# Post-norm transformer layer with a top-2 mixture of experts on one core: two more pieces of a small per-batch chain moved from VectorE to GpSimd

## The chip, the cores and the metric

One Trainium2 chip, one of its cores. The time is the kernel's device time in microseconds. The engines are named as in the profile: PE (TensorE matrix products), PEld (its weight loads), DVE (VectorE), ACT (ScalarE), POOL (GpSimd) and SP (SyncE, which issues most DMAs).

## The reference

```python
x = layernorm(x + attn(x))      # x: (4, 1024, 128), 16 heads of 8, rotary Q and K, causal softmax, W_O
p = softmax(x @ Wg + bg)        # 8 experts; the two largest are kept and divided by their sum
h = gelu(x @ W1[e] + b1[e]);  y = h @ W2[e] + b2[e]
x = layernorm(x + sum over the two experts of gate * y)
```
`layernorm(x) = (x - mean) / sqrt(var + 1e-5)`, without scale or shift. Everything is float32.

## The kernel before, in words

Tokens are handled in four batches of 1024 (`B = 4`), each as `BT = 8` tiles of 128 tokens, one token to a partition. Attention runs over 16 units: four batches, and in each four groups of four heads (`NG = 4`). A unit has 12 steps (`NB = 12`, `B_STEPS`): a step is one block of keys by up to 512 queries.

One list of events, `EVENTS` from `schedule()`, sets the order of the work on every engine: each engine walks the same list and issues its own part of each event. Behind step k of unit u stand two `QK` events (scores of the next step; PE, then ACT's exponential at L894, then on the diagonal steps 0 to 3 and 8 to 11 POOL's mask, L1499), `A` events of the next unit (a first pass over the scores: PE writes one of three PSUM banks of a ring, L723 to L728, and DVE reduces it to row maxima, L1203), and `PV` of the step before (probabilities by values, PE L778), which needs the masks of its own step. `SPLIT` cuts the row maxima into three bf16 parts on POOL (L1431 to L1437); `MT` transposes them on PE (L738). The ring has three banks, so PE can be at most three items ahead of DVE.

While the units of batch bt + 1 run, the small work that follows attention of batch bt is placed behind its steps by `after(bt)`, one event to a step. What matters here, with bt from 0 to 2 on POOL and DVE:

- `LNM`: DVE takes mean and variance pieces (`bn_stats`, L1288). `LNV`: POOL turns them into `mean` and `dev` (`moments`, L951 to L960 and L1461), behind step 9.
- `LNR` 0 and 1, behind steps 10 and 11: DVE finds `rstd = 1/sqrt(var)` with a first guess from the bits (`root_start`, L1043 and L1045) and three rounds of Newton's rule (`root_step`, L1050, L1052, L1054); one round in `LNR` 0, two in `LNR` 1. `LNR` 1 lies behind the unit's last `A` items and its `SPLIT`.
- `LNA` 0 and 1, behind steps 0 and 1 of the next unit: POOL normalises four tiles each (L998). `T2` 0 and 1, behind steps 2 and 3: PE transposes the normalised tiles (L819); `T2` c waits for `LNA` c (`x1_done`). `LG` is the gate's product (L794).
- `RD`, `RE`: POOL writes token names (L992) and running sums of the ranks (L966 to L971). `RF` 0 and 1, behind steps 4 and 5 two units on, is `place`: `RF` 0 on POOL makes each token's row for each expert (L978 to L982), `RF` 1 on DVE picks the two chosen experts' rows, with a product and a sum over eight experts each (L985, L986), and casts them (L987). `VX` copies values (L1414).
- `SC`: POOL sends the tokens to their rows in DRAM with 16 indirect DMAs (L1485), one behind each following step; the first waits for `slots_ready`.

The last batch's chain runs later, under the experts' tiles, and stays on DVE. All engines issue in order; a wait of one instruction holds all that is queued behind it on its engine. Batches 0 and 1 run in a hardware loop, batch 2 behind it.

## Time and profile before

| | us |
|---|---|
| median of 3 runs (800.60 to 803.19) | 802.84 |
| the profiled execution | 794.03 |
| its span | 792.2 |
| PE busy in the span | 661.1 (83%) |
| DVE busy | 567.6 (72%) |
| ACT busy | 442.5 (56%) |
| POOL busy | 352.9 (45%) |

The rows are from the profiled execution. The span is the stretch that the trace covers; 1.8 us of that execution's time lie outside it. Times in a row are from the span's start.

### The profile page before, as it was taken

The numbers are of one execution on the slowest core, as the hardware profiler recorded it, in microseconds if no ns is written. First come the engines' busy times: TensorE is split into PE (matmuls) and PEld (weight loads), VectorE is DVE, ScalarE is ACT, GpSimd is POOL, SyncE is SP. The second block draws the span as 40 slices with busy tenths as digits, with TensorE's granted clock in tenths as the row PEclk, the third lists the DMA queues.
The fourth block names the chain that finished last, engine by engine and source line by source line (L and its number), as shares of the span: only waits on it lengthen the run. The fifth ranks groups of instructions, "written<-read, shape, count | busy, mean of one in ns | idle before, by whom it ended". The sixth has DMA issues, their size and how long they took to land.

```text
span 792.2 us, 19057 instructions
## 1 busy us (share of the span) xinstructions
PE 661.1 (83%) x5560; PEld 355.8 (45%) x5561; DVE 567.6 (72%) x1386; ACT 442.5 (56%) x840; POOL 352.9 (45%) x664
## 2 busy tenths in 40 slices
PE   7879999999798997989999998898699666999830
PEld 3344333334343333434333334332298666889720
DVE  8977888888879886787988897986256622222266
ACT  2343667666565675456567656567467333566514
POOL 5862223323344484152447526248423654434551
PEclk9986999999999998898999999999799887999985
DMA  8883455011010120101012101000277645787923
GB/s 288 278 279 132 145 152 156 5 48 49 2 50 3 58 82 17 49 3 48 14 50 80 40 21 48 2 7 32 79 218 198 199 128 149 196 223 204 322 68 106
DMA packets 67358, 83.75 MB, mean 106 GB/s; under 512 B 9266, under 2 KB 46776, under 8 KB 67264
## 3 DMA queue, kind: packets, MB, share of 16 engines
q1 hardware_dynamic: 62912, 74.04, 31.6%
q0 software_dynamic: 4352, 8.53, 3.1%
q8 instruction: 49, 0.80, 0.4%
q14 instruction: 45, 0.37, 0.2%
HBM read 55.77 MB, written 26.90 MB: 104 GB/s over the span
## 4 chain that ended last, share of the span: by engine, by line
PE 50%; DVE 21%; issue 11%; SPq 7%; ACT 5%; POOL 2%; DMA 2%; another core or an unknown queue 1%; DVEq 0%; ACTq 0%; POOLq 0%
PE banks L778 15%; DVE mx L1203 12%; PE banks L728 9%; PE banks L758 6%; PE banks L847 4%; PE banks L836 4%; PE banks L723 3%; ACT region L894 2%; PE banks L670 2%; PE banks L787 2%; SPq L611 2%; SPq L612 2%; SPq L605 1%; DMA region<-pairs 1%
## 5 line engine op out<-in xcount | busy, mean ns | idle before, releaser
L1203 DVE TENSOR_REDUCE mx<-banks 128x1 f32<-128x512 f32 (+3 forms) x640 | 364.9, 630 | 49.9 <-PE banks L728 44.8
L894 ACT ACTIVATE region<-banks 128x1024 f32<-128x1024 f32 (+3 forms) x256 | 201.4, 841 | 134.6 <-PE banks L758 130.0
L728 PE MATMUL banks<-region 64*128 64x512 bf16 (+3 forms) x768 | 186.4, 337 | 13.6 <-DVE mx L1203 10.6
L758 PE MATMUL banks<-region 64*128 64x512 bf16 (+3 forms) x768 | 138.3, 338 | 12.4 <-ACT region L894 5.7
L778 PE MATMUL banks<-region 128*32 128x512 f32 (+3 forms) x1024 | 117.7, 533 | 0.9 <-POOL region L1499 0.8
L1509 POOL DMA_INDIRECT results<-region,dest x72 | 71.7, 995 | 102.4 <-DVE region L1335 74.7
L894 ACT ACTIVATE cs_sb<-banks 128x1024 f32<-128x1024 f32 (+2 forms) x128 | 91.0, 759 | 42.9 <-PE banks L758 42.5
L723 PE MATMUL banks<-mask_sb,half_sb 64*128 64x128 bf16 (+1 forms) x384 | 82.2, 247 | 25.2 <-DVE mx L1203 19.8
L1499 POOL TENSOR_SCALAR_AFFINE_SELECT region<-region 128x256 f32<-128x256 f32 x160 | 64.1, 409 | 82.5 <-ACT region L894 79.2
L847 PE MATMUL banks<-region,w1e 128*128 128x128 f32 x576 | 81.7, 287 | 21.0 <-ACT region L922 17.3
L1329 DVE TENSOR_TENSOR region<-banks,w1e 128x128 f32<-128x128 f32 x72 | 20.9, 291 | 108.6 <-PE banks L836 58.3
L1499 POOL TENSOR_SCALAR_AFFINE_SELECT cs_sb<-cs_sb 128x256 f32<-128x256 f32 x96 | 38.3, 410 | 127.6 <-ACT cs_sb L894 126.8
L758 PEld LDWEIGHTS banks<-region 64*128 64x128 bf16 x768 | 42.1, 94 | 111.9 <-issue 39.9
L836 PE MATMUL banks<-w_sb,region 128*128 x576 | 81.0, 285 | 4.5 <-issue 2.4
L728 PEld LDWEIGHTS banks<-region 64*128 64x128 bf16 x768 | 62.7, 97 | 49.1 <-DVE mx L1203 35.1
L847 PEld LDWEIGHTS banks<-region,w1e 128*128 128x128 f32 x576 | 74.1, 201 | 23.3 <-ACT region L922 18.9
L930 ACT ACTIVATE region<-banks,w1e 128x128 f32<-128x128 f32 x288 | 82.8, 378 | 0.5 <-PE banks L847 0.5
L836 PEld LDWEIGHTS banks<-w_sb,region 128*128 128x128 f32 x576 | 71.9, 195 | 9.1 <-issue 7.6
L1485 POOL DMA_INDIRECT pairs<-xT_sb,slot x64 | 63.2, 987 | 24.3 <-issue 14.6
L922 ACT COPY region<-banks 128x128 f32<-128x128 f32 x72 | 19.2, 267 | 90.5 <-PE banks L856 60.7
L725 PE MATMUL banks<-mask_sb,half_sb 64*128 64x64 bf16 (+1 forms) x384 | 69.2, 205 | 0.0
L723 PEld LDWEIGHTS banks<-mask_sb,half_sb 64*128 64x128 bf16 x384 | 34.6, 96 | 62.7 <-DVE mx L1203 45.5
(201 smaller groups left out, 700.8 us busy)
## 6 DMA issues: line engine op xcount, KB each, us to landing
w1e<-in_w SPq DMA_DIRECT2D x72, 322.0 KB
region<-stack_q SPq DMA_DIRECT2D x64, 112.0 KB
region<-stack_k SPq DMA_DIRECT2D x32, 224.0 KB
region<-pairs SPq DMA_DIRECT2D x72, 66.0 KB
region<-results SPq DMA_DIRECT2D x8, 512.0 KB, 4.7
stack_q<-x_sb SPq DMA_DIRECT2D x8, 384.0 KB, 3.5
stack_k<-x_sb SPq DMA_DIRECT2D x8, 384.0 KB, 4.6
stack_q<-x_sb SPq DMA_DIRECT2D x8, 256.0 KB, 3.6
```

Of the source, the lines that this page charges most:

```text
L723: mm(view[:, :, n - P:n], half_sb[rows, 0, :], mask_sb[rows, 0, 0:k, :], start=True, stop=False, skip_group_check=True)
L725: mm(view[:, :, n - P // 2:n], half_sb[rows, 1, :], mask_sb[rows, 1, 0:k, P // 2:P], start=False, stop=False, skip_group_check=True)
L728: last = mm(ring[:, bank, m * n:(m + 1) * n], qst[rows, v % NG, sb_ // 4, slot_, sb_ % 4 * P:(sb_ % 4 + 1) * P], kst[rows, v % NG, slot_, ...
L758: last = mm(score[:, slot_, par, 0:n], kst[rows, u % NG, slot_, j * P:(j + 1) * P], qst[rows, u % NG, c, slot_, s0 - c * CH:s0 - c * CH + ...
L778: last = mm(pv[32 * h:32 * h + 32, s0 - c * CH:s0 - c * CH + n], vx[:, u % NG, j, h, :], probs[(2 * e[1] + slot_) % 6][:, par, 0:n], start ...
L836: last = mm(down[k % 2], hg[:, k % 2, hc * P:(hc + 1) * P], w2_sb[:, bass.ds(e, 1), hc, :].rearrange("p a n -> p (a n)"), start=(hc == 0), ...
L847: last = mm(hidden[k % 2][:, hc * P:(hc + 1) * P], w1e[:, k, hc * P:(hc + 1) * P], xgT[:, k % 2, :], start=(hc == 0), stop=(hc == HC - 1), ...
L894: nc.scalar.activation(probs[i % 6][:, :, 0:n], score[:, i % 2, :, 0:n], ACT.Exp, scale=SCALE).then_inc(exp_done, 1)
L930: nc.scalar.activation(hg[:, k % 2, cols], hidden[k % 2][:, cols], ACT.Gelu_apprx_tanh, bias=w1e[:, k, HID + hc:HID + hc + 1]).then_inc(ge ...
L1203: read(v.tensor_reduce(dst, src, AX.X, ALU.max, negate=True))
L1499: pp.affine_select(out=block_, in_=block_, compare_op=ALU.is_ge, fill=0.0, base=0, pattern=[[0, 2], [1, P]], channel_multiplier=-1).then_i ...
L1509: pp.indirect_dma_start(out=results, out_offset=bass.IndirectOffsetOnAxis(ap=dest[:, k, :], axis=0), in_=ys[:, k, :], in_offset=None, boun ...
```

## The change

For batches 0 to 2 the Newton rounds of `LNR` 0 and 1 and the whole of `RF` 1 are issued by POOL. `root_start` stays on DVE. POOL has no fused form of the rounds here, so a round is four instructions where DVE had three; and the sum over eight experts is three additions of halves where DVE had one reduction. The counts of the semaphores `ln`, `route`, `pool_ln` and `pool_route` follow; `LNA` 0 now waits for `pool_ln`, and `TA` (tables of the experts' tiles) also for `pool_route`. The order of events is unchanged.

```diff
@@ place
                 for w in range(2):
-                    chain(v.tensor_tensor(rt[:, 8, :, :], rt[:, 6 + w, :, :], row, ALU.mult))
-                    chain(v.tensor_reduce(slot_f[:, w, :], rt[:, 8, :, :], AX.X, ALU.add))
+                    mine = rt[:, 8, :, :]
+                    chain(v.tensor_tensor(mine, rt[:, 6 + w, :, :], row, ALU.mult))
+                    if v is nc.vector:
+                        chain(v.tensor_reduce(slot_f[:, w, :], mine, AX.X, ALU.add))
+                    else:
+
+                        chain(v.tensor_tensor(mine[:, :, 0:4], mine[:, :, 0:4], mine[:, :, 4:8], ALU.add))
+                        chain(v.tensor_tensor(mine[:, :, 0:2], mine[:, :, 0:2], mine[:, :, 2:4], ALU.add))
+                        chain(v.tensor_tensor(slot_f[:, w, :], mine[:, :, 0], mine[:, :, 1], ALU.add))
                 v.tensor_copy(slot[:, :, :], slot_f[:, :, :]).then_inc(slots_ready, 1)
@@ DVE, LNR
+                    elif half == 1 and bt < B - 1:
+                        return
                     else:
                         sync()
                         if half == 0:
                             if bt < B - 1:
-                                ve.wait_ge(pool_ln, at((bt + 1) * 8, 8))
+                                ve.wait_ge(pool_ln, at(bt * POOL_LN + 8, POOL_LN))
                             root_start(rstd[:, :], dev[:, 1, :], step, sync)
-                        for _ in range(1 + half):
-                            root_step(rstd[:, :], dev[:, 1, :], nwt[:, :], step, sync)
...
@@ DVE, ROUTE_STEPS: "RF": (0, 4) becomes "RF": (0, 0)
@@ POOL
+                    elif kind == "LNR":
+                        if half == 0:
+
+                            pool.wait_ge(ln, at((bt + 1) * (BT + 2), BT + 2))
+                            pool.sem_inc(mask_turns, 1)
+                        for _ in range(1 + half):
+                            link(pp.tensor_tensor(nwt[:, :], rstd[:, :], rstd[:, :], ALU.mult))
+                            link(pp.tensor_tensor(nwt[:, :], nwt[:, :], dev[:, 1, :], ALU.mult))
+                            link(pp.tensor_scalar(nwt[:, :], nwt[:, :], -0.5, 1.5, ALU.mult, ALU.add))
+                            link(pp.tensor_tensor(rstd[:, :], rstd[:, :], nwt[:, :], ALU.mult))
...
                     if c == 0:
                         pool.wait_ge(xr_free, at(bt + 1, 1))
-                        pool.wait_ge(ln, at((bt + 1) * (BT + 11), BT + 11))
+                        pool.wait_ge(pool_ln, at((bt + 1) * POOL_LN, POOL_LN))
```

POOL's instructions at the norm of batch 2, before (`affine_select` is the mask; `L998` rows are `LNA`):

```order
L1461 TENSOR_SCALAR dev<-dev 128x8 [waits pool_ln]
L1499 AFFINE_SELECT cs_sb<-cs_sb 128x2x128 [waits exp_done] x2
L1499 AFFINE_SELECT region<-region 128x2x128 [waits exp_done] x2
L1431 TENSOR_TENSOR msp<-mx,zero 128x2x8 [waits mx_ready]
L1433 TENSOR_TENSOR mrem<-mx,msp 128x2x2x4 [waits msplit]
L1435 TENSOR_TENSOR msp<-mrem,zero 128x2x8 [waits msplit]
L1437 TENSOR_TENSOR msp<-mrem,msp 128x2x8 [waits msplit]
L1499 AFFINE_SELECT region<-region 128x2x128 [waits exp_done] x2
L998 TENSOR_SCALAR xT_sb<-y,mean,rstd 128x128 [waits xr_free,ln]
L998 TENSOR_SCALAR xT_sb<-y,mean,rstd 128x128 x3
L1499 AFFINE_SELECT cs_sb<-cs_sb 128x2x128 [waits exp_done] x2
L998 TENSOR_SCALAR xT_sb<-y,mean,rstd 128x128 x4
```

and of the change, the same place (here L1519 is the mask, L1441 to L1447 the split, L1008 the normalisation):

```order
L1519 AFFINE_SELECT cs_sb<-cs_sb 128x2x128 [waits exp_done] x2
L1478 TENSOR_TENSOR nwt<-rstd 128x8 [waits ln]
...
L1481 TENSOR_TENSOR rstd<-rstd,nwt 128x8 [waits pool_ln]
L1519 AFFINE_SELECT region<-region 128x2x128 [waits pool_ln,exp_done]
...
L1478 TENSOR_TENSOR nwt<-rstd 128x8
L1479 TENSOR_TENSOR nwt<-nwt,dev 128x8 [waits pool_ln]
...
L1481 TENSOR_TENSOR rstd<-rstd,nwt 128x8 [waits pool_ln]
L1519 AFFINE_SELECT region<-region 128x2x128 [waits pool_ln,exp_done]
...
L1008 TENSOR_SCALAR xT_sb<-y,mean,rstd 128x128 [waits xr_free,pool_ln]
```

Four instructions now stand between POOL's masks of step 11 and those of the next unit's step 0, and eight between the split and the masks of step 1, with both `LNA` behind them.

DVE's instructions at the same place before:

```order
L1045 TENSOR_SCALAR rstd<-rstd 128x8 [waits ln]
L1050 TENSOR_TENSOR nwt<-rstd 128x8 [waits ln]
L1052 SCALAR_TENSOR_TENSOR nwt<-nwt,dev 128x8 [waits ln]
L1054 SCALAR_TENSOR_TENSOR rstd<-nwt,rstd 128x8 [waits ln]
L1203 TENSOR_REDUCE mx<-banks 128x1 [waits ring_full,ln]
L1203 TENSOR_REDUCE mx<-banks 128x1 [waits ring_full]
L1207 TENSOR_TENSOR mx<-mx 128x4x4 [waits ring_read]
L1050 TENSOR_TENSOR nwt<-rstd 128x8 [waits ln]
...
L1054 SCALAR_TENSOR_TENSOR rstd<-nwt,rstd 128x8 [waits ln]
L1203 TENSOR_REDUCE mx<-banks 128x2 [waits ring_full,ln]
```

and of the change:

```order
L1053 TENSOR_SCALAR rstd<-dev 128x8 [waits pool_ln,ln]
L1055 TENSOR_SCALAR rstd<-rstd 128x8 [waits ln]
L1214 TENSOR_REDUCE mx<-banks 128x1 [waits ring_full,ln]
L1214 TENSOR_REDUCE mx<-banks 128x1 [waits ring_full]
L1218 TENSOR_TENSOR mx<-mx 128x4x4 [waits ring_read]
L1214 TENSOR_REDUCE mx<-banks 128x2 [waits ring_full] x4
L1221 COPY mparts<-banks 48x128 [waits ring_full]
```

The nine instructions of the rounds are gone; the reductions close up.

POOL's instructions at the places of batch 2 in the change (before, the first indirect DMA followed the copy directly, and the product, reduction and cast were DVE's):

```order
L985 TENSOR_TENSOR next_row<-next_row,cnt 128x8 [waits pool_route]
L1424 COPY region<-v_sb 128x32x8 [waits pool_route,vx_set,pv_done]
L989 TENSOR_TENSOR xT_sb<-xT_sb 128x64
L994 TENSOR_TENSOR xT_sb<-xT_sb 128x8x4 [waits pool_route]
L995 TENSOR_TENSOR xT_sb<-xT_sb 128x8x2 [waits pool_route]
L996 TENSOR_TENSOR slot_f<-xT_sb 128x8 [waits pool_route]
L989 TENSOR_TENSOR xT_sb<-xT_sb 128x64 [waits pool_route]
...
L996 TENSOR_TENSOR slot_f<-xT_sb 128x8 [waits pool_route]
L997 CAST slot<-slot_f 128x16 [waits pool_route]
L1505 DMA pairs<-xT_sb,slot 34816x132 [waits x1_copied,slots_ready]
```

Nine instructions stand ahead of the first indirect DMA.

## Rows read from the trace of the kernel before

**Rows 1.** Page, part 4: the chain that ended last, shares by engine.
```profile
PE 50%; DVE 21%; issue 11%; SPq 7%; ACT 5%; POOL 2%; DMA 2%; another core or an unknown queue 1%; DVEq 0%; ACTq 0%; POOLq 0%
```
**Rows 2.** Windows: PE, PEld, DVE, ACT, POOL busy us (instructions), clock, DMA share, GB/s.
```profile
228.00:338.00 110.00, 97.71 (x862) 39.41 (x862) 90.63 (x193) 66.31 (x90) 46.30 (x110) 0.95 0.13 41
...
218.20:226.10 7.90, 7.90 (x75) 3.41 (x74) 5.94 (x13) 3.23 (x6) 7.44 (x12) 0.78 0.17 48
```
**Rows 3.** Timeline, POOL, norm of batch 0: start, us, line, operation, [idle before].
```profile
212.25 0.20 POOL L960 TENSOR_TENSOR dev<-dev 128x8 f32<-128x8 f32 x1 [0.18 <-POOL dev L958]
212.64 0.20 POOL L1461 TENSOR_SCALAR dev<-dev 128x8 f32<-128x8 f32 x1 [0.20 <-POOL dev L960]
...
213.54 0.41 POOL L1499 TENSOR_SCALAR_AFFINE_SELECT region<-region 128x256 f32<-128x256 f32 x1
...
216.07 0.22 POOL L1431 TENSOR_TENSOR msp<-mx,zero 128x16 bf16<-128x16 f32 x1 [1.28 <-DVE mx L1207]
...
217.16 0.76 POOL L1499 TENSOR_SCALAR_AFFINE_SELECT region<-region 128x256 f32<-128x256 f32 x2
217.92 3.15 POOL L998 TENSOR_SCALAR xT_sb<-y,mean,rstd 128x128 f32<-128x128 f32 x4
...
221.79 3.12 POOL L998 TENSOR_SCALAR xT_sb<-y,mean,rstd 128x128 f32<-128x128 f32 x4
```
**Rows 4.** Timeline, DVE, the same stretch.
```profile
213.29 0.33 DVE L1045 TENSOR_SCALAR rstd<-rstd 128x8 int32<-128x8 int32 x1
213.65 0.32 DVE L1050 TENSOR_TENSOR nwt<-rstd 128x8 f32<-128x8 f32 x1
...
214.49 1.29 DVE L1203 TENSOR_REDUCE mx<-banks 128x1 f32<-128x512 f32 x2
...
215.91 0.16 DVE L1050 TENSOR_TENSOR nwt<-rstd 128x8 f32<-128x8 f32 x1
...
217.24 1.95 DVE L1203 TENSOR_REDUCE mx<-banks 128x2 f32<-128x256 f32 x4
```
**Rows 5.** Timeline, PE: transposes of the row maxima, and of `LNA` 0 and 1.
```profile
218.56 0.26 PE L738 MATMUL banks<-idb_sb,msp 128*96 128x128 bf16 x1
...
224.17 0.60 PE L819 MATMUL banks<-id_sb,xT_sb 128*128 128x128 f32 x4
...
226.10 0.66 PE L819 MATMUL banks<-id_sb,xT_sb 128*128 128x128 f32 x4
```
**Rows 6.** Chain in order of time, behind the second transpose.
```profile
226.17 0.59 PE banks L819 x4
...
228.22 0.69 DVE mx L1203
```
**Rows 7.** Timeline, POOL and PE, the norm of batch 2.
```profile
484.89 3.13 POOL L998 TENSOR_SCALAR xT_sb<-y,mean,rstd 128x128 f32<-128x128 f32 x4
...
489.12 0.66 PE L819 MATMUL banks<-id_sb,xT_sb 128*128 128x128 f32 x4
```
**Rows 8.** Timeline, all engines, the places of batch 0.
```profile
263.62 0.32 POOL L981 TENSOR_TENSOR xT_sb<-xT_sb,next_row 128x64 f32<-128x64 f32 x1 [0.18 <-POOL xT_sb L980]
...
264.11 0.21 POOL L982 TENSOR_TENSOR next_row<-next_row,cnt 128x8 f32<-128x8 f32 x1 [0.18 <-POOL xT_sb L981]
...
264.72 0.40 POOL L1414 COPY region<-v_sb 128x256 f32 x1 [0.40 <-POOL next_row L982]
...
265.97 0.21 DVE L985 TENSOR_TENSOR xT_sb<-xT_sb 128x64 f32<-128x64 f32 x1
...
267.07 2.49 DVE L1203 TENSOR_REDUCE mx<-banks 128x1 f32<-128x512 f32 x4
...
267.82 0.28 PE L723 MATMUL banks<-mask_sb,half_sb 64*128 64x256 bf16 x1 [0.90 <-DVE mx L1203]
...
268.12 1.21 POOL L1485 DMA_INDIRECT pairs<-xT_sb,slot  x1 [3.00 <-DVE slot L987]
...
271.60 0.40 POOL L1499 TENSOR_SCALAR_AFFINE_SELECT cs_sb<-cs_sb 128x256 f32<-128x256 f32 x1 [2.27 <-ACT cs_sb L894]
```

More of the change, by code:

```diff
@@ L454, in build @@
         pool_ln = sem("pool_ln")
-        POOL_ROUTE = 13
+        POOL_STEPS = {("LNV", 0): 0, ("LNR", 0): 8, ("LNR", 1): 12,
+                      ("RD", 1): 0, ("RE", 0): 2, ("RE", 1): 5, ("RF", 0): 9, ("RF", 1): 13}
+        POOL_LN, POOL_ROUTE = 20, 21
         spare_in = sem("spare_in")
@@ L1110, in early_tiles @@
                 ve.wait_ge(route, 2 + (B - 1) * PER_ROUTE)
+                ve.wait_ge(pool_route, (B - 1) * POOL_ROUTE)
                 chain(v.tensor_tensor(n_e, next_row[:, :], first_row_sb[:, :], ALU.subtract))
@@ L1175, in late_tiles @@
                                            tile_at[:, EARLY:NTILE], ALU.mult, ALU.add).then_inc(tiles_ready, 1)
-            ROUTE_STEPS = {"RA": (1,), "RS": (3,), "RB": (3, 3), "RC": (3, 2), "RD": (5, 0), "RE": (0, 0), "RF": (0, 4)}
+            ROUTE_STEPS = {"RA": (1,), "RS": (3,), "RB": (3, 3), "RC": (3, 2), "RD": (5, 0), "RE": (0, 0), "RF": (0, 0)}
             LAST_STEPS = {**ROUTE_STEPS, "RD": (5, 2), "RE": (3, 4), "RF": (4, 4)}
             PER_ROUTE = sum(sum(n) for n in ROUTE_STEPS.values())
-            PER_LN = BT + 5 + 6
+            PER_LN = BT + 2
             def visit(e, r, at):
@@ L1265, in visit @@
                     else:
-                        if bt < B - 1:
-                            ve.wait_ge(pool_route, at((bt + 1) * POOL_ROUTE, POOL_ROUTE))
                         place(v, half, link_route)
@@ L1276, in visit @@
                     bt, half = e[1:]
-                    done = [bt * PER_LN + {"LNM": half * BT // 2, "LNV": BT, "LNR": BT + (bt == B - 1) * 8 + half * 5}[kind]]
+                    done = [bt * PER_LN + {"LNM": half * BT // 2, "LNV": BT, "LNR": BT + (bt == B - 1) * (8 + half * 5)}[kind]]
                     def step(ins):
@@ L1298, in visit @@
                             if bt < B - 1:
-                                ve.wait_ge(pool_ln, at((bt + 1) * 8, 8))
+                                ve.wait_ge(pool_ln, at(bt * POOL_LN + 8, POOL_LN))
                             root_start(rstd[:, :], dev[:, 1, :], step, sync)
-                        for _ in range(1 + half):
-                            root_step(rstd[:, :], dev[:, 1, :], nwt[:, :], step, sync)
-                    if kind == "LNR" and half == 1:
-                        assert done[0] == (bt + 1) * PER_LN + (bt == B - 1) * 8
+                        if bt == B - 1:
+                            for _ in range(1 + half):
+                                root_step(rstd[:, :], dev[:, 1, :], nwt[:, :], step, sync)
                 elif kind == "TA":
@@ L1437, in visit @@
                     pp.tensor_tensor(part[2], rest, part[1], ALU.subtract).then_inc(msplit, 1)
-                elif e[0] in ("LNV", "RD", "RE", "RF") and e[1] < B - 1 and (e[0] in ("LNV", "RE") or e[2] == (e[0] == "RD")):
+                elif e[0] in ("LNV", "LNR", "RD", "RE", "RF") and e[1] < B - 1 and (e[0], *e[2:]) != ("RD", 0):
                     kind, bt, half = e
-                    turn, per, first = (pool_ln, 8, 0) if kind == "LNV" else (
-                        pool_route, POOL_ROUTE, {("RD", 1): 0, ("RE", 0): 2, ("RE", 1): 5, ("RF", 0): 9}[kind, half])
+                    turn, per = (pool_ln, POOL_LN) if kind in ("LNV", "LNR") else (pool_route, POOL_ROUTE)
+                    first = POOL_STEPS[kind, half]
                     done = [bt * per + first]
@@ L1456, in visit @@
                     if kind == "LNV":
-                        pool.wait_ge(ln, at(bt * (BT + 11) + BT, BT + 11))
+                        pool.wait_ge(ln, at(bt * (BT + 2) + BT, BT + 2))
                         pool.sem_inc(mask_turns, 1)
@@ L1461, in visit @@
                         step(pp.tensor_scalar(dev[:, 1, :], dev[:, 0, :], 1.0 / D, EPS, ALU.mult, ALU.add))
+                    elif kind == "LNR":
+                        if half == 0:
+                            pool.wait_ge(ln, at((bt + 1) * (BT + 2), BT + 2))
+                            pool.sem_inc(mask_turns, 1)
+                        for _ in range(1 + half):
+                            link(pp.tensor_tensor(nwt[:, :], rstd[:, :], rstd[:, :], ALU.mult))
+                            link(pp.tensor_tensor(nwt[:, :], nwt[:, :], dev[:, 1, :], ALU.mult))
+                            link(pp.tensor_scalar(nwt[:, :], nwt[:, :], -0.5, 1.5, ALU.mult, ALU.add))
+                            link(pp.tensor_tensor(rstd[:, :], rstd[:, :], nwt[:, :], ALU.mult))
                     elif kind == "RD":
```

## The prediction

> **What bounds the kernel now.** I read the page's chain of work first. PE holds half of it and DVE a fifth, POOL 2% [rows 1]: through attention PE and DVE take turns, tied by the ring of three banks, and between two norms PE is busy 97.71 and DVE 90.63 of 110 us [rows 2]. Neither has much idle time in which a delay could be made up. So I read the two places of the change in order of time on POOL, DVE and PE, and ask at each which engine is waited for.
>
> At the norm of batch 0 DVE's rounds lie in front of reductions that PE waits for. One round runs from 213.65 to the next reduction at 214.49, two from 215.91 to 217.24 [rows 4]: 0.84 and 1.33 us, 2.17 in all. POOL meanwhile waits 1.28 us before its split at 216.07, and from there it is without a gap: split, masks, four normalisations from 217.92 to 221.07, masks, four more from 221.79 to 224.91 [rows 3]. PE transposes the second four at 226.10 [rows 5], 1.19 us after POOL is done with them. That 1.19 us is all the cover that POOL's queue has there. In the chain in order of time that transpose is PE's own, and behind it come PE's gate product, scores and first pass, and then DVE's reduction at 228.22 [rows 6]. A delay of the transpose is a delay of what follows.
>
> At the places of batch 0 DVE's five instructions run from 265.97 to 267.07, and PE has waited 0.90 us for the reduction behind them when it goes on at 267.82 [rows 8]. POOL has been done with its copy since 265.12 and waits for the cast; its first indirect DMA starts at 268.12, its next mask at 271.60 [rows 8].
>
> **The change part by part. 1. DVE loses nine instructions at each norm.** They are on the path: PE could go on up to 2.17 us sooner, so taken alone this is worth up to 6.5 us in three batches. The price of DVE's dropped register and wait work is in those gaps already.
>
> **2. POOL gains four instructions behind the masks of step 11.** POOL has no Newton round in this trace. The nearest rows are the last steps of the variance, same size (128x8), same engine, same kind of wait behind each: 0.20 us long, but 212.25 to 212.64 from start to start [rows 3], 0.39 us. I price a step at 0.40. The multiply-add and the last step are of the same kind. `root_start` ends at 213.62 [rows 4]; four steps from 213.7 end, wait included, at 215.3. The pair of masks that stood at 213.54 and behind then takes 0.75 us, to 216.05. The split stood at 216.07 and had waited 1.28 us for DVE. DVE is now earlier, POOL is not: the split stays where it was. So these four steps cost nothing, covered by that 1.28 us and by the gap between the two masks; they also use up all of it, so DVE's earlier maxima bring POOL nothing. What the masks hold up, PE's products of the next unit's step 0, comes behind 218.56 [rows 5].
>
> **3. POOL gains eight instructions behind the split.** They depend on each other: 8 x 0.40 = 3.2 us. Queued behind them are the masks of step 1, `LNA` 0, the masks of step 2, `LNA` 1, the masks of step 3. No idle time stands between these before [rows 3], so all shift by 3.2: `LNA` 0 ends at 224.25 instead of 221.07, `LNA` 1 at 228.1 instead of 224.91. PE came to the first transpose at 224.17 and to the second at 226.10 [rows 5]. The first is hardly later than before, though PE comes sooner and waits. The second goes from 226.10 to 228.2, 2.1 us later than before. In batch 2 the same sum gives 484.89 + 3.13 + 3.2 = 491.2 against 489.12 [rows 7], again 2.1; batch 1 lies like batch 0. Hence the gain of part 1 is gone, eaten by waits of PE between 217 and 228, and 3 x 2.1 = 6.3 us are lost on top. Bounds: if POOL's steps followed each other at their length alone (0.20), the eight would take 1.6 and the transpose be 0.4 late, 1.2 us in all; if each took 0.5, as POOL's 128x64 step does from start to start (263.62 to 264.11) [rows 8], 4.0 us, a lateness of 2.9, 8.7 in all. I take 0.40, whose rows have the size and the waits of the new steps.
>
> The Trainium skill bears on this choice: Perfetto Trace Analysis, section GPSIMD Engine Instruction, says that a GpSimd span in a profile is unreliable and that such instructions should be timed from start to start. By spans the three batches would lose 1.2 us, by starts 6.3; the trace agrees with the page in so far as its start-to-start time is twice the span [rows 3].
>
> **4. The places.** DVE loses 1.10 us (265.97 to 267.07). PE's own work ends at about 266.9, 0.90 us before it goes on [rows 8], so 0.9 of it is a gain, 2.7 us in three batches (bounds 0, if another wait takes its place, and 3.3). POOL gains nine instructions. Two products of 128x64 at 0.49 from start to start, two sums of 32 at about 0.45 (between the rows for 64 and for 8 elements, as an estimate), four more at 0.40, a cast of 0.2: 3.7 us [rows 3, 8]. From 265.12 they end near 268.8, 1.7 us later than DVE's cast. The indirect DMA follows by 0.97 us as before and takes 1.21 [rows 8]: it ends near 271.0, ahead of the mask that stood at 271.60 and comes at 270.7 now. The mask is some 0.3 us late; its product on PE is some steps away. So it costs nothing; without that cover it would be 0.3 a batch.
>
> **5. Semaphores.** `TA` waits for `pool_route` too, which was met long before. Nothing.
>
> **The sum.** +6.3 - 2.7 = +3.6 us on the profiled execution's 794.03, so 797.6. The median of the runs shown, 802.84, is 8.8 above that execution; the change is the same number of microseconds on it: 806.4. A measurement here can tell about 0.3%, 2.4 us, from no change.
>
> **The rivals.**
> **A. The forecast**: PE's second transpose waits for `LNA` 1, the places gain. +2.4 to +6.5 us, 805.2 to 809.3. Chance 0.50.
> **B. The clock makes it worse.** In the 7.9 us up to the second transpose PE's granted clock was 0.78 [rows 2]: a mix of 2.4 and 1.2 GHz, about 3.5 us at the lower level (0.22 x 2 x 7.9), behind DVE's rounds and PE's waits for them. Those 3.5 us now lie in time that PE waits anyway. But PE's new waits come later, up to 228.2, and if the lower level moves behind the transpose it costs up to half of 3.5, 1.7 us a batch. For it: from 216.2 to 228.2 PE has about 6.2 us of work at full clock (0.78 x 7.9), so it idles half of the time. Against: from 228 to 338, with 12 us of PE's waits in it, the clock is 0.95 on the mean [rows 2]. +3.6 + 5.2 = +8.8, 811.6. Chance 0.17.
> **C. POOL's steps are as short as their spans**, or the chain is otherwise short: +1.2 - 2.7 = -1.5, 801.3. Also here, with the same time, that PE's part behind the transpose has slack of its own. Chance 0.15.
> **D. Faster: the lateness is recovered.** The 2.1 us arise at one place; the next place where this chain matters is 40 us later. If DVE, not PE, sets the pace in between, the ring fills while PE waits, and PE's lateness is absorbed by the 12 us that PE is idle in 110 [rows 2]. Then only the places count: -2.7, 800.1. It decides for "faster" if fewer than 0.1 us of each 2.1 are left. Against it: during the wait DVE has nothing to reduce either, since PE issues the first pass behind the transpose, and the chain there is all PE. Chance 0.11.
> **E. The work moved, but the path doesn't notice**: PE waits elsewhere for the same things. Within 2.4 us of 802.8. Chance 0.07.
>
> **How the numbers follow.** Slower holds A and B, 0.67, and a little of C and E's tails, 0.69. Within 0.3% are most of C and E and the edge of A: 0.18. Faster is D and the tail of C, 0.13. The range leaves out the far end of B and of D: 800.6 to 811.5. A's own range is 805.2 to 809.3.
>
> **What the changed profile would show.** POOL: four L1478 to L1481 steps near 213.7, 0.4 apart; the split still near 216.1; eight steps to 220.4; `LNA` 1 ending near 228.1. PE: waits at the masks of step 1 and at both transposes, the second released by POOL's L1008, near 228.2 in the time of before. DVE: reductions without a gap from 213.65, then idle between 221 and 228. At the places: PE's 0.90 us wait gone, the first indirect DMA near 269.8. Right size: the start of the same step of batch 1 later by 1.2 us than before. The prediction is wrong if PE's second transpose is not released by POOL, if the steps' spacing is not 0.4, or if the distance from that transpose to the places shrinks.

## The result and the profile after

The changed kernel takes 810.85 us (median of 4 runs, 810.06 to 814.17) against 801.78 us (4 runs, 800.60 to 803.19) for the kernel before in the same comparison. The ratio is 1.0127, 95% interval [1.0087, 1.0166]: slower by 7 to 13 us, where +3.6 us was forecast. The profiled execution took 810.95 us, with a span of 809.1.

The page of the changed kernel, busy time and chain of work (the lines that answer to [rows 1] and the small table):
```profile
PE 680.4 (84%) x5560; PEld 368.1 (45%) x5561; DVE 562.6 (70%) x1344; ACT 443.7 (55%) x840; POOL 366.4 (45%) x727
...
PE 51%; DVE 17%; issue 9%; SPq 5%; ACT 5%; POOL 5%; another core or an unknown queue 3%; DMA 2%; POOLq 0%; DVEq 0%; ACTq 0%
```
DVE's share of the chain fell from 21 to 17%, as its instructions left. POOL's rose from 2 to 5%. PE is busy 19 us longer with the same number of matmuls, and its mean granted clock is 0.913 instead of 0.933; the windows below show where it was lower.

POOL of the changed kernel in order of time, norm of batch 0 (start, us, line, [idle before]). All that stands here is 3.96 us late already when the norm begins (DVE's L1055 starts at 217.24, its counterpart of before at 213.29 [rows 4]); those 3.96 us arose between 45 and 75 us, ahead of every edit of the change, where the changed kernel's clock was at its lower level for 34 us in all and that of the kernel before for 17. Other kernels below show between -0.2 and +4.4 there whatever was edited. The 3.96 us are taken off in what follows.
```profile
217.75 0.20 POOL L1478 TENSOR_TENSOR nwt<-rstd 128x8 f32<-128x8 f32 x1 [0.21 <-DVE rstd L1055]
218.13 0.20 POOL L1479 TENSOR_TENSOR nwt<-nwt,dev 128x8 f32<-128x8 f32 x1 [0.18 <-POOL nwt L1478]
...
219.58 0.76 POOL L1519 TENSOR_SCALAR_AFFINE_SELECT region<-region 128x256 f32<-128x256 f32 x2 [0.33 <-POOL rstd L1481]
220.31 0.22 POOL L1441 TENSOR_TENSOR msp<-mx,zero 128x16 bf16<-128x16 f32 x1
...
221.37 0.20 POOL L1478 TENSOR_TENSOR nwt<-rstd 128x8 f32<-128x8 f32 x1
...
224.06 0.20 POOL L1481 TENSOR_TENSOR rstd<-rstd,nwt 128x8 f32<-128x8 f32 x1 [0.18 <-POOL nwt L1480]
224.58 0.76 POOL L1519 TENSOR_SCALAR_AFFINE_SELECT region<-region 128x256 f32<-128x256 f32 x2 [0.33 <-POOL rstd L1481]
225.34 3.15 POOL L1008 TENSOR_SCALAR xT_sb<-y,mean,rstd 128x128 f32<-128x128 f32 x4
...
229.21 3.11 POOL L1008 TENSOR_SCALAR xT_sb<-y,mean,rstd 128x128 f32<-128x128 f32 x4
```
The split starts at 220.31, less 3.96 that is 216.35, against 216.07 [rows 3]: where it stood. The steps are 0.38 us apart, from 221.37 to 224.06 in seven of them. The second normalisation ends at 232.32 - 3.96 = 228.36.

PE of the changed kernel, its waits in the same stretch:
```profile
221.47 0.33 PE L741 MATMUL banks<-idb_sb,msp 128*96 128x128 bf16 x1 [0.96 <-POOL msp L1447]
...
228.55 0.66 PE L822 MATMUL banks<-id_sb,xT_sb 128*128 128x128 f32 x4 [1.30 <-POOL xT_sb L1008]
...
232.38 0.66 PE L822 MATMUL banks<-id_sb,xT_sb 128*128 128x128 f32 x4 [1.77 <-POOL xT_sb L1008]
```
Both transposes are released by POOL, and the second starts at 228.42 in the time of before, 2.32 us later than at 226.10 [rows 5].

And the chain of the changed kernel in order of time, through the second transpose:
```profile
226.93 1.56 POOL xT_sb L1008 x2
228.49 0.73 POOL cs_sb L1519 x2
229.22 3.12 POOL xT_sb L1008 x4
232.33 0.04 issue
232.38 0.66 PE banks L822 x4
233.03 0.79 PE banks L797 x8
```
POOL's queue carries the chain where it was PE's own before [rows 6].

What the forecast left out lies behind that transpose. Windows of the changed kernel (columns as in [rows 2]): the stretch with the two waits, then one behind the second transpose of each of the three batches:
```profile
226.00:232.40 6.40, 3.32 (x32) 1.38 (x24) 3.21 (x7) 2.03 (x4) 6.40 (x11) 1.00 0.40 129
235.20:242.00 6.80, 6.76 (x40) 3.54 (x40) 4.64 (x9) 3.57 (x5) 1.27 (x5) 0.50 0.01 1
368.30:378.50 10.20, 10.20 (x58) 5.83 (x57) 6.05 (x12) 6.04 (x7) 1.49 (x6) 0.50 0.00 0
501.40:511.60 10.20, 10.20 (x56) 4.47 (x53) 5.95 (x14) 5.07 (x7) 1.22 (x5) 0.50 0.01 2
```
and of the kernel before: its stretches at the lower level ahead of the norm's transposes in batches 0 and 1, and what it does where the changed kernel is slow:
```profile
219.00:222.40 3.40, 3.40 (x30) 1.16 (x26) 1.80 (x5) 1.42 (x4) 3.40 (x6) 0.50 0.04 8
229.00:235.80 6.80, 6.32 (x59) 3.28 (x63) 6.25 (x15) 5.62 (x8) 1.27 (x5) 1.00 0.08 28
352.10:355.50 3.40, 3.40 (x32) 1.55 (x30) 2.76 (x6) 1.70 (x3) 3.40 (x6) 0.50 0.01 2
365.80:372.60 6.80, 6.72 (x33) 1.97 (x33) 5.03 (x12) 3.33 (x5) 0.00 (x0) 0.50 0.02 4
489.50:499.70 10.20, 9.37 (x83) 4.80 (x81) 8.81 (x19) 8.70 (x11) 1.22 (x5) 1.00 0.14 45
```
PE is busy 3.32 of 6.40 us up to the second transpose, at a granted clock of 1.00; then, with PE full of work again, the clock is 0.50, that is 1.2 GHz, for 6.8, 10.2 and 10.2 us. In 10.2 us PE gets through 56 matmuls where it did 83.

To see where each microsecond arose I matched the matmuls of L778 (L781 in the changed kernel), probabilities by values, one by one in the order in which they run: 1536 in either trace. The shift is the start in one trace minus the start in the trace of before. Times on the left are those of before.

| changed kernel, shift in us | norm 0 | norm 1 | norm 2 |
|---|---|---|---|
| ahead of the norm (212.6, 346.6, 475.9) | 3.96 | 5.44 | 8.32 |
| at the second transpose | 6.27 | 7.87 | 10.66 |
| 14 to 25 us behind it (240.2, 385.5, 511.9) | 8.73 | 9.06 | 14.37 |
| ahead of and behind the places | 8.58, 7.88 | 8.92, 8.21 | 14.37, 13.67 |

So in these two traces a norm costs 2.31, 2.43 and 2.34 us up to the transpose, 7.1 in all, and 2.46, 1.19 and 3.71 behind it, 7.4 in all. In batch 1 the kernel before has a stretch at the lower level of its own there (365.80, above), worth 2.45 us (by so much run 3's shift falls there, and nothing else of it changes). The places give back 0.70 each, 2.1 us. Sum: +12.3 us, inside the measured 7 to 13. Not in this sum is a stretch between the norms: from 300 to 334 the shift of the changed kernel falls by 2.5 us, and that of run 2 below, whose norm is DVE's, by 3.0. There the kernel before was at the lower level for 10.2 us (from 311.1), the changed one for 6.8 (from 317.1). Over the whole stretch from 212.6 to 540 the shift grows by 9.7 us. How much of the 7.4 us belongs to this pair of executions alone is taken up behind the last experiment.

### The profile page after: what moved, and what is told of

Read it like the earlier page. It is cut to its first block, busy times and chain, and to the rows that moved or that the text cites. A ratio compares the mean times of both kernels' runs of the same rounds, so it can differ in the third digit from the quotient of the medians.

```text
span 809.1 us, 19151 instructions
## 1 busy us (share of the span) xinstructions
PE 680.4 (84%) x5560; PEld 368.1 (45%) x5561; DVE 562.6 (70%) x1344; ACT 443.7 (55%) x840; POOL 366.4 (45%) x727
## 4 chain that ended last, share of the span: by engine, by line
PE 51%; DVE 17%; issue 9%; SPq 5%; ACT 5%; POOL 5%; another core or an unknown queue 3%; DMA 2%; POOLq 0%; DVEq 0%; ACTq 0%
PE banks L781 14%; DVE mx L1214 11%; PE banks L731 9%; PE banks L761 6%; PE banks L850 4%; PE banks L839 4%; PE banks L673 3%; ACT region L897 3%; PE banks L726 3%; POOL xT_sb L1008 2%; PE banks L790 2%; PE banks L688 2%; SPq L614 2%; SPq L608 1%
## 5 line engine op out<-in xcount | busy, mean ns | idle before, releaser
L731 PE MATMUL banks<-region 64*128 64x512 bf16 (+3 forms) x768 | 191.2, 347 | 11.6 <-DVE mx L1214 8.9
L761 PE MATMUL banks<-region 64*128 64x512 bf16 (+3 forms) x768 | 140.1, 341 | 11.3 <-ACT region L897 5.5
L781 PE MATMUL banks<-region 128*32 128x512 f32 (+3 forms) x1024 | 118.7, 537 | 1.9 <-POOL region L1519 1.8
L1519 POOL TENSOR_SCALAR_AFFINE_SELECT region<-region 128x256 f32<-128x256 f32 x160 | 63.6, 408 | 86.0 <-ACT region L897 81.8
L850 PE MATMUL banks<-region,w1e 128*128 128x128 f32 x576 | 84.2, 293 | 19.8 <-ACT region L925 11.9
L1519 POOL TENSOR_SCALAR_AFFINE_SELECT cs_sb<-cs_sb 128x256 f32<-128x256 f32 x96 | 38.0, 408 | 127.6 <-ACT cs_sb L897 126.6
L839 PE MATMUL banks<-w_sb,region 128*128 x576 | 83.8, 291 | 4.2 <-issue 2.1
L850 PEld LDWEIGHTS banks<-region,w1e 128*128 128x128 f32 x576 | 76.8, 207 | 22.1 <-ACT region L925 13.5
L839 PEld LDWEIGHTS banks<-w_sb,region 128*128 128x128 f32 x576 | 74.6, 201 | 8.8 <-issue 7.7
```

The source lines that it names most:

```text
L731: last = mm(ring[:, bank, m * n:(m + 1) * n], qst[rows, v % NG, sb_ // 4, slot_, sb_ % 4 * P:(sb_ % 4 + 1) * P], kst[rows, v % NG, slot_, ...
L761: last = mm(score[:, slot_, par, 0:n], kst[rows, u % NG, slot_, j * P:(j + 1) * P], qst[rows, u % NG, c, slot_, s0 - c * CH:s0 - c * CH + ...
L781: last = mm(pv[32 * h:32 * h + 32, s0 - c * CH:s0 - c * CH + n], vx[:, u % NG, j, h, :], probs[(2 * e[1] + slot_) % 6][:, par, 0:n], start ...
L839: last = mm(down[k % 2], hg[:, k % 2, hc * P:(hc + 1) * P], w2_sb[:, bass.ds(e, 1), hc, :].rearrange("p a n -> p (a n)"), start=(hc == 0), ...
L850: last = mm(hidden[k % 2][:, hc * P:(hc + 1) * P], w1e[:, k, hc * P:(hc + 1) * P], xgT[:, k % 2, :], start=(hc == 0), stop=(hc == HC - 1), ...
L1519: pp.affine_select(out=block_, in_=block_, compare_op=ALU.is_ge, fill=0.0, base=0, pattern=[[0, 2], [1, P]], channel_multiplier=-1).then_i ...
```

## The experiments

Theories on record with them: **C** (clock), the second transpose is late by POOL's eight steps, and PE's waits for it bring a stretch at 1.2 GHz behind it that costs as much again; **W**, the extra is another wait that POOL's queue brings. All ratios are to the kernel before on the same chip, with 95% intervals. "Shift" is that of the table above. The diffs are excerpts: the semaphore counts that follow an edit are left out.

**1. The rounds on POOL alone.** `RF` 1 goes back to DVE:
```diff
-            ROUTE_STEPS = {"RA": (1,), "RS": (3,), "RB": (3, 3), "RC": (3, 2), "RD": (5, 0), "RE": (0, 0), "RF": (0, 0)}
+            ROUTE_STEPS = {"RA": (1,), "RS": (3,), "RB": (3, 3), "RC": (3, 2), "RD": (5, 0), "RE": (0, 0), "RF": (0, 4)}
```


> Only the Newton rounds are POOL's; the places' second half is DVE's again. Theory C (the clock): the second transpose of each norm comes 2.3 us late, and the lower PE clock that follows PE's waits costs a further 1.3 to 3.7 us behind it. So all of the loss and 2.1 us more: 809 + 2 = about +11 us against the kernel before (1.012 to 1.016). Theory W (a further wait, not the clock, and partly from the places on POOL): the norm alone costs the 6.3 us of the recorded sum, +6 us (1.008), with the lower clock no longer than before.

Measured: 814.95 us, ratio 1.0188 [1.0148, 1.0229], 12 to 18 us slower. Shifts: -0.19, 2.11 and 6.17 at norm 0; 5.03, 7.44, 8.59; 8.65, 11.25, 14.63; nothing at the places. The loss is the norm's. The ratio lies above what theory C expected (1.012 to 1.016), and its interval reaches into it; lateness and extra behind the transposes add up to 7.3 + 8.6 us in the trace.

**2. The places on POOL alone.** The rounds go back to DVE.

> Only the places' second half is POOL's; the Newton rounds are DVE's again. Both theories: DVE drops 1.1 us a batch, of which PE gets 0.7, so -2.1 us (0.997), the norms as in the kernel before. If the places add a hidden cost (the rival that blames them), the ratio is 1.00 or above.

Measured: 798.27 us, ratio 0.9934 [0.9900, 0.9969]. The shift falls by 0.71, 0.71 and 0.70 at the three places, 2.1 us; the ratio says 2.5 to 8. The two parts add up: 1.0188 and 0.9934 make 1.0122, the whole is 1.0127. The ratio gives more than the 2.1 us that can be seen; by the medians, 798.27 against 800.54, it is 2.3. The norms, though, are not as in the kernel before, as was expected: at norm 0 this kernel's shift grows by 4.0 us (3.98 to 7.95), with DVE's rounds and no wait of PE at either transpose. Windows of this kernel, ahead of the second transpose of norm 0 (231.54) and through it, then behind it:
```profile
228.70:235.50 6.80, 6.44 (x65) 3.84 (x57) 5.09 (x11) 4.85 (x6) 1.73 (x7) 1.00 0.35 118
235.50:242.30 6.80, 6.80 (x36) 3.00 (x36) 4.07 (x11) 3.47 (x5) 0.44 (x2) 0.50 0.01 2
```
So a stretch at the lower level behind the transpose, worth 2.5 us (5.44 to 7.95), comes without POOL's steps too, in one of three norms here as in the kernel before. A stretch there is by itself no proof of theory C; how often it comes, and what filling PE's waits does to it, has to decide.

**3. One round on POOL, two on DVE**, where POOL's four steps lie under cover and none stands behind the split:
```diff
-                elif e[0] in ("LNV", "LNR", "RD", "RE", "RF") and e[1] < B - 1 and (e[0], *e[2:]) != ("RD", 0):
+                elif e[0] in ("LNV", "LNR", "RD", "RE", "RF") and e[1] < B - 1 and (e[0], *e[2:]) not in (("RD", 0), ("LNR", 1)):
```


> First Newton round on POOL (the four steps that POOL's idle time covered), rounds two and three on DVE, places on POOL. If part 2 of the prediction is right that four steps are covered: the second transpose is not late, DVE gains 0.84 us at each norm and PE 0.7 at each of the places: -3 to -4.5 us (0.994 to 0.996). If four steps already cost, it is slower than e2.

Measured: 794.72 us, ratio 0.9921 [0.9890, 0.9953], a little faster than the expected 0.994 to 0.996. The second transposes are not late (shifts 2.58 to 2.30, -1.63 to -1.81, -4.92 to -4.97), and behind them there is no stretch at the lower level. DVE in that trace:
```profile
217.65 0.17 DVE L1218 TENSOR_TENSOR mx<-mx 128x16 f32<-128x16 f32 x1
217.93 0.17 DVE L1060 TENSOR_TENSOR nwt<-rstd 128x8 f32<-128x8 f32 x1
218.13 0.17 DVE L1062 SCALAR_TENSOR_TENSOR nwt<-nwt,dev 128x8 f32<-128x8 f32 x1
218.33 0.32 DVE L1064 SCALAR_TENSOR_TENSOR rstd<-nwt,rstd 128x8 f32<-128x8 f32 x1
218.68 0.33 DVE L1060 TENSOR_TENSOR nwt<-rstd 128x8 f32<-128x8 f32 x1
```
DVE now waits for POOL's round until 217.93 and two of its steps take twice as long, so of the 0.84 us that the first round had cost [rows 4] at most 0.3 are won (0.28, 0.18 and 0.05 at the three norms). This is the fastest kernel here, but not measurably faster than the one with the places alone.

**4. PE kept at work while it waits.** The changed kernel, with matmuls whose result nobody reads ahead of the transposes, into the bank that the transposes then fill:
```diff
                     else:
+                        if bt < B - 1:
+                            for _ in range((5, 7)[c]):
+                                mm(ring[:, bank, :], idb_sb[:, :], mask_sb[:, :, :, :].rearrange("p a b n -> p (a b n)"),
+                                   start=True, stop=True, skip_group_check=True)
                         pe.wait_ge(x1_done, at(2 * bt + c + 1, 2))
```


> The changed kernel with 5 and 7 products without use (bf16, 512 columns, into the bank that the transpose then overwrites) ahead of the two transposes that wait for the norm, in batches 0 to 2. They fill PE's waits of 1.3 and 1.8 us and take no time from other work. Theory C: the clock stays at 2.4 GHz behind the transpose, and each norm loses 2.3 us instead of 3.6 to 6.1: +5 us against the kernel before (1.005 to 1.007), 4 to 7 us below the changed kernel. Theory W: as the changed kernel, or slower by the filling.

Measured: 805.29 us, ratio 1.0040 [1.0011, 1.0070]. More work for PE and 0.87% faster than the changed kernel. The second transpose is as late as before (2.32, 2.43, 2.25 us), as it must be, since POOL does the same. Behind it:
```profile
233.20:240.00 6.80, 6.80 (x35) 2.65 (x36) 4.37 (x12) 3.04 (x4) 0.06 (x1) 0.50 0.02 4
366.90:377.10 10.20, 9.32 (x84) 5.19 (x84) 8.38 (x18) 8.19 (x10) 1.98 (x7) 1.00 0.02 6
499.50:506.30 6.80, 6.80 (x36) 2.66 (x36) 4.29 (x12) 3.02 (x4) 0.00 (x0) 0.50 0.01 2
```
In batch 1 the clock stays at 1.00 and nothing is lost behind the transpose (6.97 to 4.53, the 2.45 us being the slow stretch of the kernel before); in batches 0 and 2 it is at 0.50 for 6.8 us, and 2.1 and 2.3 us are lost. POOL does the same, the transposes are as late, and only PE's idle time is filled: what is won came with the clock. This speaks for C and against W.

**5 and 6. Four steps behind the split, and twelve.** The number of rounds in `LNR` 1 is the dose; the third round is left out in the first, and a fourth is added in the second.
```diff
-                        for _ in range(1 + half):
+                        for _ in range((1) if half else 1):
```
and
```diff
-                        for _ in range(1 + half):
+                        for _ in range((3) if half else 1):
```


> The changed kernel with one Newton round in the second part instead of two: four steps behind the split, not eight (the third round is left out, so the norm's root is less exact). A step is 0.39 us and the eight made the second transpose 2.35 us late, so four make it 0.8 us late. Theory C (the loss is PE's wait and the lower clock that follows it): +2.4 us for the waits, less of the lower clock behind them, -2.1 us at the places: 0.999 to 1.006. Theory W: the loss does not follow the number of steps, 1.01.

> The changed kernel with three rounds in the second part (one round more than is needed): twelve steps behind the split. The second transpose 3.9 us late, 11.7 us in three norms, the lower clock behind each for 7 to 10 us at 0.35 us lost per us (+8 to 10 us), -2.1 us at the places: 1.02 to 1.026. Theory W: as the changed kernel plus 4.7 us at most, 1.018 or less.

Measured: 801.52 us, ratio 1.0029 [1.0003, 1.0056], and 815.18 us, 1.0212 [1.0180, 1.0244]. The second transpose is late by 0.8, 0.9 and 1.1 us with four steps, 3.93, 4.03 and 3.93 with twelve: 0.36 to 0.39 us a step, queued one behind the other. The extra behind it doesn't follow the dose. Windows of the kernel with four steps:
```profile
233.90:240.70 6.80, 6.67 (x40) 3.53 (x40) 4.72 (x10) 3.67 (x5) 1.27 (x5) 0.50 0.01 1
367.00:377.20 10.20, 10.20 (x56) 4.45 (x53) 5.95 (x14) 5.01 (x7) 1.27 (x5) 0.50 0.01 3
496.80:507.00 10.20, 10.20 (x55) 5.05 (x54) 6.05 (x12) 5.64 (x7) 1.22 (x5) 0.50 0.02 5
```
and with twelve:
```profile
227.50:244.60 17.10, 15.65 (x80) 8.10 (x80) 7.80 (x15) 8.46 (x9) 7.07 (x15) 0.50 0.11 38
360.60:384.50 23.90, 22.05 (x123) 11.17 (x127) 11.40 (x24) 10.85 (x14) 12.62 (x34) 0.50 0.13 40
```
With a third to a half of the lateness the stretches are as long as in the changed kernel. With more of it those of batches 0 and 1 begin ahead of the transpose, run through the wait and beyond, and add 4.5 and 1.4 us behind the transpose; that of batch 2 (500.6 to 507.4) ends at the transpose (507.46), and nothing is lost behind it. The trace of the kernel with four steps adds up to 2.8 us of lateness and 7.1 behind, less 2.1 at the places, 7.8 us; its time is only 0.2 to 4.5 us above the kernel before. So the extra that one trace shows does not carry over to the median of twelve executions.

**7 and 9. The transposes one step later.** `T2` and all that follows it in the chain of batches 0 to 2 move by one step, so that POOL has time; `SW` joins the last `SC`. First in the changed kernel, then as its control in the kernel with the places alone.
```diff
-            [("LNA", bt, 0)], [("LNA", bt, 1)], [("T2", bt, 0)], [("T2", bt, 1), ("XC", bt), ("LG", bt, 0)], [("LG", bt, 1)],
+            [("LNA", bt, 0)], [("LNA", bt, 1)], *([[]] if bt < B - 1 else []), [("T2", bt, 0)], [("T2", bt, 1), ("XC", bt), ("LG", bt, 0)], [("LG", bt, 1)],
```


> The changed kernel with the two transposes of batches 0 to 2, and all that follows them in the chain, one step later in the list. PE then has a step's work, some 3 us, to do while POOL normalises. Theory C: no wait of PE at the transposes, only short ones for POOL's masks, less of the lower clock, the places still -2.1 us: 0.996 to 1.003. If what costs is POOL's queue as such (masks of steps 1 to 3 late), it stays at 1.01.

> This is the kernel with only the places on POOL (rounds of the root on DVE, as before), with T2 and all that follows it for batches 0 to 2 one step later, as in the run e7_transposes_later. It is the control for that run: no POOL steps at the norm, so no wait is taken away here, and what it costs against e2_places_only (0.9934 [0.9900, 0.9969]) is the price of the later order by itself. If the order costs nothing (what I had assumed for e7): 0.990 to 0.997, as e2. If the later order meets DVE at busier places and so ate e7's gain: 1.002 to 1.008, about 7 to 12 us more than e2, since e7 stayed within 0.2% of the changed kernel's ratio while its second transposes had stopped waiting. Between these, 0.997 to 1.002, it explains half of it. By the theory of the clock e7's second transposes no longer wait in any case, so this run does not bear on it directly; it says whether e7 counts against it. In the trace the stretch from 16 to 50 us behind the transposes should grow by 2 to 3 us against e2 if the order costs, by under 0.5 us if not.

Measured: 809.71 us, ratio 1.0110 [1.0066, 1.0153], and 803.82 us, 1.0058 [1.0030, 1.0086]. The first missed its expectation, and I took it for evidence against C until the control ran. PE in the trace of the first:
```profile
228.13 0.64 PE L781 MATMUL banks<-cs_sb,region 128*32 128x256 f32 x8 [1.24 <-POOL cs_sb L1519]
...
228.70 0.66 PE L822 MATMUL banks<-id_sb,xT_sb 128*128 128x128 f32 x4
...
231.97 0.43 PE L781 MATMUL banks<-region 128*32 128x128 f32 x8 [0.82 <-POOL region L1519]
...
232.33 0.66 PE L822 MATMUL banks<-id_sb,xT_sb 128*128 128x128 f32 x4
```
The transposes wait for nothing any more, and up to 359.4 and 488.5 in batches 1 and 2 the norm costs nothing (6.08 to 6.02, 9.15 to 8.93). But the later order costs by itself: the control is 1.24% above the kernel with the places alone, 10 us, and its shift grows by 2.7, 2.8 and 3.0 us where the chain behind the transposes now meets other steps (240.2 to 261.9, 385.5 to 400.9, 511.9 to 524.3). In each of the three the control has 6.8 us at the lower level, and the kernel with the places alone has none; the first is
```profile
257.70:264.50 6.80, 6.80 (x54) 3.26 (x54) 4.74 (x15) 2.55 (x5) 1.77 (x5) 0.50 0.11 26
```
Against its control the first kernel loses 0.5%, some 4 us, for the rounds on POOL (the two intervals leave 0 to 1%); without the later order they cost 1.93%, 15 us (1.0127 less 0.9934). So most of the loss does hang on the transposes' wait.

**8. Eight steps of POOL elsewhere.** The kernel with the places alone, and eight chained 128x8 products behind the masks of step 3, where POOL is idle:
```diff
+                elif e[0] == "T2" and e[1] < B - 1:
+                    bt, c = e[1:]
+                    if c == 0:
+                        for i in range(8):
+                            pp.tensor_tensor(spare[:, :], spare[:, :], spare[:, :], ALU.mult).then_inc(extra, 1)
+                            pool.wait_ge(extra, at(bt * 8 + 2 + i, 8))
...
```


> The kernel of e2 (places on POOL, Newton rounds on DVE) with eight steps of the same size without use on POOL, chained in the same way, behind the masks of step 3, where POOL idled 3.35 us. If the position in POOL's queue is what costs, the 3.2 us are free: as e2, 0.992 to 0.997. If POOL's added work costs wherever it stands (a port shared with DVE, masks late), it is 1.5 to 6 us slower than e2.

Measured: 794.59 us, ratio 0.9949 [0.9920, 0.9979], as the kernel without them. Eight such steps cost nothing where nobody waits for POOL's queue:
```profile
232.28 0.20 POOL L1495 TENSOR_TENSOR spare<-spare 128x8 f32<-128x8 f32 x1 [0.18 <-POOL spare L1495]
234.51 0.22 POOL L1442 TENSOR_TENSOR msp<-mx,zero 128x16 bf16<-128x16 f32 x1 [2.03 <-DVE mx L1216]
```
After the last of them POOL still waits 2.03 us for DVE. It is the place of the steps that costs, not their number.

**10. PE kept at work at the row maxima too.** Run 4 with four more such matmuls ahead of the transpose of the row maxima:
```diff
+                    if v % NG == 0 and v > 0 and c == 1:
+                        for _ in range(4):
+                            mm(ring[:, bank, :], idb_sb[:, :], mask_sb[:, :, :, :].rearrange("p a b n -> p (a b n)"),
+                               start=True, stop=True, skip_group_check=True)
                     pe.wait_ge(msplit, at(8 * v + 4 * c + 4, 8 * NG))
```


> The changed kernel with useless matmuls of PE ahead of both transposes of each norm (5 and 7, as in e4_pe_kept_busy, 1.0040) and 4 more ahead of the transpose of the row maxima (MT of the second pair, at the first unit of batches 1 to 3), where PE waits 0.96 us for POOL's split. The output is the same. Theory of the clock: the wait at MT is the first of the three in a row that bring the lower level behind them; filled too, the stretches at the lower level behind the second transposes (6.8 us in batches 0 and 2 in e4) become shorter or vanish, and 0 to 5 us are won against e4: 0.998 to 1.004. If the level depends on nothing that PE does at these places, it stays at e4's 1.0040 or gets slower by the few tenths of a us that the extra matmuls stick out, 1.004 to 1.007. If the second transpose waits on POOL by as much as before (0.15 us behind seven matmuls in e4), the lateness of 2.3 us a batch itself stays in both cases.

Measured: 803.27 us, ratio 1.0037 [1.0007, 1.0068]: the time can't be told from run 4's 1.0040. The profiled execution shows two of the three norms without a slow stretch behind the transpose:
```profile
234.70:241.50 6.80, 6.80 (x36) 2.66 (x36) 4.28 (x11) 2.91 (x4) 0.13 (x1) 0.50 0.01 4
367.70:377.90 10.20, 9.37 (x84) 5.15 (x84) 8.46 (x19) 8.21 (x10) 1.92 (x7) 1.00 0.02 5
496.00:506.20 10.20, 9.37 (x84) 5.16 (x84) 8.44 (x19) 8.25 (x10) 1.88 (x7) 1.00 0.01 2
```
There the second transpose is 2.50 and 2.32 us late and at most 0.2 us come on top (7.69 to 5.23 with the 2.45 of before, 6.86 to 7.03); in batch 0, with 6.8 us at 0.50, it is 2.2 us. That is C once more, norm by norm; that the wait at the row maxima is one that brings the clock down is not shown by the times.

**The clock over all executions.** One trace is one execution, and the clock differs between executions of one kernel: over 75 of the kernel before it was 0.913 to 0.938 on the mean of an execution, the time 793.5 to 805.6 us. From clock and span follows the time at the lower level, 2 x (1 - clock) x span; means over executions, in us:

| kernel (executions) | at 1.2 GHz | lateness of the three second transposes |
|---|---|---|
| before (75); the profiled one alone 106 | 120 | |
| changed (4) | 134 | 7.1 |
| run 1, rounds alone (6) | 140 | 7.3 |
| run 5, four steps (12) | 120 | 2.8 |
| run 6, twelve steps (6) | 152 | 11.9 |
| runs 4 and 10, PE's waits filled (12 each) | 111, 108 | 7.0, 7.2 |
| run 2, places alone, rounds on DVE (12) | 115 | |

With the lateness unchanged and PE's waits filled, the level that had come with them is gone, and 0.87% of the time with it: this is what shows C. By norms of the profiled executions, a stretch at 1.2 GHz lies behind the second transpose in 11 of 12 where it comes behind POOL's added steps (changed, runs 1, 5, 6), in 3 of 6 with the waits filled, and in 3 of 12 where PE waits for neither transpose (before, runs 2, 3, 8). For the size: among executions of the kernel before, 1 us more at the lower level goes with 0.24 us more of time. Some 14 us more of it in the changed kernel (four executions, 125 to 143 us) would then be 3.4 us, at the traces' 0.36 us 5.0. As an estimate the clock so costs 3 to 5 us on the median, not the 7.4 of the one pair of traces, whose kernel before was an execution with little of the lower level. With 7.1 of lateness less 2.1 at the places that makes 8.4 to 10.0 us; the medians are 9.1 apart.

## Why the prediction was right or wrong

The direction and the place were right; the size was not. Step by step:

**1. DVE's nine instructions.** They left, and PE's waits took up what DVE gave, as the prediction had it. Shown by the shift, which first falls (3.96 to 1.88 at 218.2) and then rises to 6.49 at 229.3.

**2. The four steps behind the masks cost nothing.** Right: the split stayed within 0.3 us, and run 3, which has these four alone, loses nothing at the norm.

**3. The eight steps behind the split.** The price of a step, 0.40 from start to start, was right (0.38 in the changed kernel, 0.36 to 0.39 from four steps to twelve). The Trainium skill, Perfetto Trace Analysis, section GPSIMD Engine Instruction, advises the start-to-start spacing over the span, and here the dose agrees: by spans of 0.20 eight more steps from run 5's four to run 6's twelve would add 1.6 us of lateness, measured were 2.9 to 3.1. The lateness was 2.1 forecast, 2.3 to 2.4 measured, 7.1 us in all instead of 6.3; 0.3 us of it is the split. That the delay isn't made up later was right: rival D fell, and so did C and E. The sign of its right size, 1.2 us between one step of batch 1 and the same step before, was too small: the shift stands at 7.98 near 300, 4.0 above where it stood ahead of norm 0. And the prediction guarded against a distance from transpose to places that shrinks; it grew, by 2.3 us (6.27 to 8.58).

**The step that failed** is the sum's silence on what comes behind the transpose: it priced the lateness at itself, gave the clock nothing, and put it into rival B, with "1.7 us a batch" and a chance of 0.17. B was the case that came. Of the 5.5 us by which the change of the medians, 9.1, exceeds the forecast 3.6, the lateness explains 0.8 (7.1 instead of 6.3) and the places 0.6 (2.1 instead of 2.7); what is left, 4.1 us, is the term that was missing. In the pair of traces it is 2.5 to 3.7 us a norm where the kernel before has no such stretch, 7.4 us in all; over all executions 3 to 5 us, as an estimate. B's own 5.2 us lies between these, but that is in part luck, for its size came from a wrong reading of [rows 2]. I had taken its 3.5 us at the lower level for a fixed amount that would move. But the stretch in front stayed in batches 0 and 1 (221.5 to 224.9 and 358.0 to 361.5 in the changed kernel) and went in batch 2 only, and new ones of 6.8 to 10.2 us came behind PE's waits of 1.30 and 1.77. My argument against B, that the clock is 0.95 from 228 to 338 in spite of PE's 12 us of waits, looked at waits strewn over 110 us; here two stand within 6.4 us, and PE works 3.32 of these. Each microsecond at the lower level cost about 0.36 us (2.46 for 6.8, 3.71 for 10.2). Why that is less than the half that it could cost PE is not shown; behind the norm of batch 2 the kernel before leaves PE idle for 0.83 of 10.20 us, which would take up a part.

**4. The places.** 0.9 us each were forecast, 0.70 were seen. POOL's nine instructions took 3.6 us (273.65 to 277.25) against the 3.7 forecast, and the first indirect DMA stands at 278.22, in the time of before 269.6 to 270.3 against "near 269.8".

**5. Semaphores.** No wait of `TA` came into the chain.

The prediction carried its change over from an execution of 794.03 us to a median of 802.84 as if the two differed in nothing that matters. They differ in the clock as well: 0.933 in the profiled execution, 0.925 on the mean of the others, some 14 us less at the lower level and by 0.24 us each 3.4 of the 8.8 us. For the forecast's own sum, a difference without the clock, that did no harm; for reading the loss from one pair of traces it did.

## What to carry to other kernels

Work that goes from a waited-for engine to one with spare time is paid by what queues behind it there: eight small steps made PE 2.3 us late behind the split, and cost nothing behind the masks of step 3. The Trainium skill, Perfetto Trace Analysis, section Optimizing Scalar/DVE Operations, allows such moves when DVE is saturated and doubts them over the read port that GpSimd and DVE share; here the place in the queue decided. Whether DVE's slow steps beside POOL's masks (run 3) are that port's doing no run shows. And where an edit makes PE wait one or two microseconds more, look at the granted clock behind the waits, and price a stretch at 1.2 GHz there next to the wait itself: here it came to about half of the wait's own cost over all executions and to as much again in one pair of traces, and useless matmuls in PE's idle time gave 0.87% back. Such a stretch comes and goes between executions of one kernel, so hold the mean granted clock of several against it before a trace's microseconds are taken for the cost. An experiment that moves a chain in time needs the same move in a kernel without the suspected cause beside it, or its own cost is taken for the answer.

## What I had not expected of the hardware

- The length of the slow stretch didn't follow the length of the wait: behind a second transpose 0.8 to 1.1 us late it was 6.8 to 10.2 us, as behind one 2.3 us late. PE's wait for it was near the same in both, 1.77 us; in two of run 5's norms it was the only one of the two transposes' waits, and the stretches were 10.2 us all the same. What sets the length stays open, and so does why one came at norm 0 of runs 2 and 8 and at norm 1 of the kernel before, where PE waits for neither transpose.
- The lower level can cover the wait as well as what follows (run 6), and then costs less than its length suggests: in batch 0 it lasted 17.1 us, and the shift behind the transpose grew by 4.5; in batch 2 it ended at the transpose and cost nothing behind it.
- DVE's 128x8 steps of the rounds took 0.32 instead of 0.17 us beside POOL's masks (run 3, its two rounds 1.60 instead of 1.33 us). Beside POOL's 128x8 and 128x16 steps they stayed at 0.17 to 0.22. The trace of before had it too, 0.32 beside the mask at 213.54 and 0.16 where POOL waits [rows 3, 4], and I had not read it as a cost of putting the two side by side.
